# A two-layer LSTM scan with attention: the gates' biases written into PSUM by ScalarE instead of by nine bias matmuls a step

## The reference, cut to what matters

```
def _lstm_cell(x, h, c, Wi, Wh, bi, bh):
    g = x @ Wi.T + bi + h @ Wh.T + bh
    i, f, gg, o = jnp.split(g, 4, axis=-1)
    c2 = jax.nn.sigmoid(f) * c + jax.nn.sigmoid(i) * jnp.tanh(gg)
    h2 = jax.nn.sigmoid(o) * jnp.tanh(c2)
    return (h2, c2)
...
def step(carry, x_t):
    h0, c0, h1, c1, a = carry
    xin = jnp.concatenate([x_t, a], axis=-1)
    h0, c0 = _lstm_cell(xin, h0, c0, Wi0, Wh0, bi0, bh0)
    h1, c1 = _lstm_cell(h0, h1, c1, Wi1, Wh1, bi1, bh1)
    q = h1 @ Wq.T
    attn = jax.nn.softmax(jnp.einsum('bh,bsh->bs', q, context), axis=-1)
    mixed = jnp.einsum('bs,bsh->bh', attn, context)
    a2 = jnp.tanh(jnp.concatenate([mixed, h1], axis=-1) @ Wo.T + bo)
    return ((h0, c0, h1, c1, a2), a2)
```

## Time and profile before

| | |
|---|---|
| median of three runs | 8625.89 us |
| the profiled execution's own time | 8623.44 us |
| its span, first to last instruction | 8621.7 us |
| TensorE matmuls busy | 7757.2 us (90% of the span), 389701 instructions |
| VectorE busy | 4295.5 us (50%) |
| ScalarE busy | 2528.3 us (29%) |
| mean granted clock of TensorE | 0.969 |

### The profile page before, as it was taken

How to read it: one execution, slowest core, us unless ns; L and a number is a source line. 1 busy time by engine, 2 the same in 40 slices (tenths; PEclk the granted TensorE clock), 3 DMA queues, 4 the chain that set the end, 5 groups by cost and what they waited for, 6 DMA issues and landing times. The chain is left out here.

```text
span 8621.7 us, 829171 instructions
## 1 busy us (share of the span) xinstructions
PE 7757.2 (90%) x389701; PEld 6261.9 (73%) x389709; DVE 4295.5 (50%) x21178; ACT 2528.3 (29%) x12971; POOL 281.7 (3%) x295
## 2 busy tenths in 40 slices
PE   7999999999999999999999999999999999576677
PEld 5777777777777777777777777777777777353455
DVE  5444444444444444444444444444444444557712
ACT  2222222222222222222222222222222222223322
POOL 0000000000000000000000000000000000113411
PEclk8999999999999999999999999999999999798788
DMA  1000000000000000000000000000000000000233
GB/s 51 0 0 0 0 0 0 0 0 0 0 0 0 0 0 0 0 0 0 0 0 0 0 0 0 0 0 0 0 0 0 0 0 0 25 15 8 102 117 113
DMA packets 61677, 92.70 MB, mean 11 GB/s; under 512 B 13976, under 2 KB 50248, under 8 KB 60744
## 3 DMA queue, kind: packets, MB, share of 16 engines
q1 hardware_dynamic: 58568, 83.84, 2.9%
q0 software_dynamic: 3072, 8.39, 0.3%
HBM read 73.34 MB, written 18.87 MB: 11 GB/s over the span
## 5 line engine op out<-in xcount | busy, mean ns | idle before, releaser
L334 PE MATMUL scan_sums_ig<-rec_wh,scan_hT 128*8 128x64 f32 x65504 | 1291.2, 219 | 2.8 <-issue 2.8
L334 PEld LDWEIGHTS scan_sums_ig<-rec_wh,scan_hT 128*8 128x8 f32 x65504 | 1026.8, 90 | 3.2 <-issue 3.2
L456 DVE STREAM_TRANSPOSE scan_sums_f<-scan_sums_f 128x64 f32<-128x64 f32 x2048 | 543.3, 265 | 837.0 <-PE scan_sums_f L334 837.0
L405 ACT ACTIVATE scan_tanh_f<-scan_sums_f 128x8 f32<-128x8 f32 x2048 | 362.8, 177 | 1827.2 <-DVE scan_sums_f L456 1827.2
L334 PE MATMUL scan_sums_o<-rec_wh,scan_hT 128*4 128x64 f32 x32752 | 833.9, 219 | 3.0 <-issue 3.0
L334 PE MATMUL scan_sums_f<-rec_wh,scan_hT 128*4 128x64 f32 x32752 | 833.5, 219 | 0.0
L456 DVE STREAM_TRANSPOSE scan_sums_ig<-scan_sums_ig 128x64 f32<-128x64 f32 x2048 | 543.5, 265 | 372.2 <-PE scan_sums_ig L334 372.2
L334 PE MATMUL scan_sums_ig<-rec_wa,scan_aT 128*8 128x64 f32 x32768 | 646.7, 219 | 0.0
L334 PE MATMUL scan_sums_ig<-rec_wx,scan_xT 128*8 128x64 f32 x32768 | 645.8, 219 | 0.0
L334 PE MATMUL scan_sums_ig<-rec_wi,scan_hT 128*8 128x64 f32 x32768 | 645.0, 219 | 0.0
L419 ACT ACTIVATE scan_aT<-scan_a_sum 128x8 f32<-128x8 f32 x1024 | 181.5, 177 | 1510.6 <-DVE scan_a_sum L484 1510.6
(11 more groups left out here) (291 smaller groups left out, 14243.4 us busy)
## 6 DMA issues: line engine op xcount, KB each, us to landing
experts_bias<-in_b SPq DMA_DIRECT2D x40, 640.0 KB, 3.8
moe_w<-in_w SPq DMA_DIRECT2D x16, 1024.0 KB, 12.5
slots_x<-route_zero SPq DMA_DIRECT2D x40, 128.0 KB, 1.7
experts_x<-slots_x SPq DMA_DIRECT2D x40, 128.0 KB, 2.0
slots_y<-experts_y SPq DMA_DIRECT2D x40, 128.0 KB, 1.7
front_x<-in_x_steps SPq DMA_DIRECT2D x32, 128.0 KB, 2.0
w_xres<-in_x SPq DMA_DIRECT2D x4, 1024.0 KB, 9.8
out<-w_xres SPq DMA_DIRECT2D x8, 512.0 KB, 3.0
```

The lines of the kernel that those rows point to most:

```text
L334: last = nc.tensor.matmul(sums[layer][BANK[g]][32 * j:32 * j + ROWS[g], 0:64], state[:, k, FIRST[g]:FIRST[g] + ROWS[g]], weight[:, k, j, 6 ...
L405: nc.scalar.activation(tanh_f[l][:], gates_of[l][F][:, :, 0:B], ACT.Tanh).then_inc(f_tanh[l], 1)
L456: nc.vector.transpose(turned[l][g], sums[l][g][:, 0:64]).then_inc(gates_turned[l][g], 1)
```

## The change

The selection matrices, the bf16 parts and all nine seeds of a step are taken out. The three banks of a layer become one PSUM tensor, and ScalarE copies the layer's biases, laid out by the host in the shape of the sums (zero where no gate has a row), into the first 64 columns of all three banks with one instruction (`seed`). It does so right after its last tanh of the layer, once `hT` of that layer is there. TensorE waits for that copy (`seeded`) ahead of `wh1` and of `wh0`. Before the first step, six matmuls of zeros mark the banks as written, so that later products add onto ScalarE's data. The output's bias is added to `vp` once, in `prepare_scan` (the softmax's weights sum to one). With the seeds gone, `wx` of the input and cell gates also stands ahead of `vp`; only `wx` of the output gate is left behind it.

```diff
-                sp.wait_ge(rows_zeroed, 3)
-                for p in range(3):
-                    rows = slice(32 * p, 32 * p + 4)
-                    for l in range(2):
-                        gates = slice(BIAS_AT[l], BIAS_AT[l] + GATES)
-                        sp.dma_start(bias[0][rows, gates, :], ins[f"bi{l}"]).then_inc(bias_in, 16)
-                        sp.dma_start(bias[1][rows, gates, :], ins[f"bh{l}"]).then_inc(bias_in, 16)
-                    sp.dma_start(bias[0][rows, GATES, :], ins["bo"]).then_inc(bias_in, 16)
+                for l in range(2):
+                    for tile, name in ((bias[0], f"bi{l}"), (bias[1], f"bh{l}")):
+                        sp.dma_start(tile[:, l, :, :], ins[name]).then_inc(bias_in, 16)
+                sp.dma_start(bo[:], ins["bo"].partition_broadcast(P)).then_inc(bias_in, 16)
...
-                dve.wait_ge(bias_in, 16 * 15)
+                dve.wait_ge(bias_in, 16 * 5)
...
-                nc.vector.tensor_copy(w["bias_parts"][:], bias[0][:]).then_inc(parts, 1)
...
+                for at, gates in ((0, slice(0, 1)), (2, slice(3, 4))):
+                    nc.vector.tensor_scalar(w["bias"][:, :, at:at + 1, :], bias[0][:, :, gates, :], 0.5, None, ALU.mult).then_inc(scaled, 1)
+                nc.vector.scalar_tensor_tensor(w["bias"][:, :, 1, :], bias[0][:, :, 1, :], 0.5, bias[0][:, :, 2, :],
+                                               ALU.mult, ALU.add).then_inc(scaled, 1)
...
-                    nc.vector.tensor_copy(w["vp"][:, k, :, :].rearrange("p j u -> p (j u)"),
-                                          vp[k][:, 0:D]).then_inc(scaled, 1)
-                dve.wait_ge(scaled, 23)
+                    nc.vector.tensor_tensor(w["vp"][:, k, :, :].rearrange("p j u -> p (j u)"), vp[k][:, 0:D], bo[:],
+                                            ALU.add).then_inc(scaled, 1)
...
-        sums = [[m.psum(f"sums{l}_{g}") for g in ("f", "ig", "o")] for l in range(2)]
+        layer_sums = [m.psum(f"sums{l}", (P, 3, 512)) for l in range(2)]
+        sums = [[t[:, g, :] for g in range(3)] for t in layer_sums]
...
-                def seed_bias(bank, at, rows=w["sel"], start=True):
-
-                    nc.tensor.matmul(bank[:, 0:64], rows[:], bias_parts[:, 64 * at:64 * at + 64], start=start, stop=False,
-                                     skip_group_check=True)
-
-                def seed_gates(layer):
-                    at = BIAS_AT[layer]
-                    seed_bias(sums[layer][F], at + GATE_F)
-                    seed_bias(sums[layer][IG], at + GATE_I)
-                    seed_bias(sums[layer][O], at + GATE_O)
-                    seed_bias(sums[layer][IG], at + GATE_G, w["sel_high"], False)
...
+                    pe.wait_ge(seeded[1], n)
                     product(1, hT[1], w["wh1"])
                     pe.wait_ge(h_ready[0], n + 1)
                     product(1, hT[0], w["wi1"], done=gates_summed[1])
                     if not last:
-                        seed_gates(0)
+                        pe.wait_ge(seeded[0], n + 1)
                         product(0, hT[0], w["wh0"], (GATE_F, GATE_I, GATE_G))
                     pe.wait_ge(h_ready[1], n + 1)
                     head_product(scores, state_of(hT[1]), w["kp"], True, True).then_inc(scores_done, 1)
-                    seed_bias(a_sum, GATES)
-                    head_product(a_sum, state_of(hT[1]), w["woh"], False, False)
+                    head_product(a_sum, state_of(hT[1]), w["woh"], True, False)
                     if not last:
                         product(0, hT[0], w["wh0"], (GATE_O,))
-                        seed_gates(1)
                         pe.wait_ge(x_ready, n + 1)
-                        product(0, xT[(s + 1) % 2], w["wx"], (GATE_F,))
+                        product(0, xT[(s + 1) % 2], w["wx"], (GATE_F, GATE_I, GATE_G))
                     pe.wait_ge(probs_ready, n)
                     head_product(a_sum, pT[:], w["vp"], False, True).then_inc(a_summed, 1)
                     if not last:
-                        product(0, xT[(s + 1) % 2], w["wx"], (GATE_I, GATE_G, GATE_O))
+                        product(0, xT[(s + 1) % 2], w["wx"], (GATE_O,))
                 pe.wait_ge(zeroed, 1)
-                seed_gates(0)
-                seed_gates(1)
+                for l in range(2):
+                    for bank in sums[l]:
+                        last = nc.tensor.matmul(bank[:, 0:64], w["ident"][:], zeros[:], start=True, stop=True, skip_group_check=True)
+                    last.then_inc(opened, 1)
+                pe.wait_ge(seeded[0], 1)
                 pe.wait_ge(x_ready, 1)
                 product(0, xT[0], w["wx"])
                 with pe.Fori(0, T // U - 1) as i:
...
+                def seed(l, n):
+
+                    act.wait_ge(h_ready[l], n)
+                    nc.scalar.activation(layer_sums[l][:, :, 0:64], w["bias"][:, l, :, :], ACT.Copy).then_inc(seeded[l], 1)
...
                         nc.scalar.activation(tanh_c[l], c_of[l], ACT.Tanh).then_inc(h_factors[l], 1)
+                        seed(l, n + 1)
...
-                act.wait_ge(zeroed, 1)
+                act.wait_ge(opened, 2)
+                for l in range(2):
+                    seed(l, 1)
...
+    def bias_rows(bias):
+
+        rows = np.zeros((4, 32, GATES, 64), bias.dtype)
+        for g, first in enumerate((0, 0, B, 0)):
+            rows[:, first:first + B, g, :] = gate_blocks(bias)[g][:, None, :]
+        return rows.reshape(P, GATES, 64)
```

More of the change, by code:

```diff
@@ L120, in prepare_scan @@
         ctx_split = m.sbuf("ctx_split", [P, KC, 2, P])
[L122 to L125, removed]
+        bias = [m.sbuf(f"bias{i}", [P, 2, GATES, 64]) for i in range(2)]
+        bo = m.sbuf("bo", [P, D])
         kp = [m.psum(f"kp{k}") for k in range(2)]
         vp = [m.psum(f"vp{k}") for k in range(2)]
-        zeroed, ident_done, rows_zeroed = m.sem("zeroed"), m.sem("ident_done"), m.sem("rows_zeroed")
+        zeroed, ident_done = m.sem("zeroed"), m.sem("ident_done")
         fold_in, scan_in, bias_in = m.sem("fold_in"), m.sem("scan_in"), m.sem("bias_in")
-        folded, scaled, parts = m.sem("folded"), m.sem("scaled"), m.sem("parts")
+        folded, scaled = m.sem("folded"), m.sem("scaled")
         with nc.Block() as block:
@@ L159, in _ @@
                                             channel_multiplier=1).then_inc(zeroed, 1)
[L161 to L164, removed]
                 pool.wait_ge(zeroed, 6)
@@ L312, in scan @@
         xT = [m.sbuf(f"xT{i}", [P, 2, 3 * B]) for i in range(2)]
+        zeros = m.sbuf("zeros", [P, 64])
         state_of = lambda tile: tile[:, :, B:2 * B]
@@ L323, in scan @@
                                "inv_done", "a_turned", "a_kept", "zeroed"))
+        opened = m.sem("opened")
+        seeded = [m.sem(f"seeded{l}") for l in range(2)]
         with nc.Block() as block:
@@ L326, in _ @@
             def _(pe):
-                bias_parts = w["bias_parts"][:].rearrange("p g u -> p (g u)")
                 def product(layer, state, weight, gates=(GATE_F, GATE_I, GATE_G, GATE_O), done=None):
@@ L446, in _ @@
                     nc.vector.memset(tile[:], 0.0)
+                nc.vector.memset(zeros[:], 0.0)
                 nc.vector.memset(scores[:, 0:S], 0.0)
@@ L1531, in build @@
                         r[name] = m.sbuf(name, [P, 2, 4, 64])
-                    r["bias_parts"] = m.sbuf("bias_parts", [P, BIASES, 64], BF16)
-                    r["sel"] = m.sbuf("sel", [P, P], BF16)
-                    r["sel_high"] = m.sbuf("sel_high", [P, P], BF16)
+                    r["bias"] = m.sbuf("bias", [P, 2, 3, 64])
                     r["off_rows"] = m.sbuf("off_rows", [P, 1])
@@ L1609, in lay_out @@
         "woh": wo[:, D:].reshape(4, 64, 4, 2, 32).transpose(2, 4, 3, 0, 1).reshape(P, 2, 4, 64),
-        "bo": a["L0_xattn_bo"].reshape(4, 64),
+        "bo": a["L0_xattn_bo"],
         "w_in": chunked(a["L0_ffn_W_in"].T),
@@ L1624, in lay_out @@
     for name in ("bi0", "bh0", "bi1", "bh1"):
-        out[name] = bias_blocks(a[f"L0_xattn_{name}"])
+        out[name] = bias_rows(a[f"L0_xattn_{name}"])
     return {k: np.ascontiguousarray(v) for k, v in out.items()}
```

8 lines of the change are left out of this document (1 added, 7 removed).

## The result

The changed kernel took 8551.06 us (median of four runs, 8549.21 to 8551.91) against 8628.57 us (8621.46 to 8632.06): a ratio of 0.991, with a 95% interval of 0.9895 to 0.9926. 8545 was forecast.

A forecast was written before the change was run, and what follows sets the result against it. The recurrence was taken to bound the kernel, not TensorE. From the profiled 8623.4 us, 77 for covered branches and 3 for preparation and start gave 8543, stated as 8545 us; own range 8532 to 8560, 8-in-10 range 8528 to 8608.

The forecast's parts named there:

- What bounds the kernel: Scan: the recurrence's chain sets a step's length, not TensorE; removing the seeds by itself puts 0 on the path.
- The branch: TensorE's loop end: uncovered branch makes aT wait, 0.151 us each; moving wx ahead of vp covers it fully.
- The size: Scan: 511 branches at 0.151 us each, 77 us saved; 55 us by the skill's 108 ns.
- ScalarE's copies: Scan, after each layer's last tanh: about 0.35 us each, covered, cost 0 unless a copy took over 0.72 us.
- Preparation and start: Ahead of the first step: -3 us together, bounds -5 to 0, with zero matmuls and two copies adding some 1 us.
- VectorE's part: Preparation: VectorE's work on the biases shrinks to 1.5 us for all, 4 us less.
- The room ahead of `vp`: TensorE between kp and vp: with two more wx gates, loads end by 4006.43 against vp at 4006.87, covered by 0.4 us.
- VectorE's branch: VectorE's loop end behind a_hist: taken as covered; if late by up to 0.15 us, it eats up to the whole gain.
- Their writes: Rival, chance 0.04: ScalarE's writes hold TensorE during copies; whole-copy holds add 717 us, about 9260; 0.037 us each undoes the gain.
- The clock: Rival, chance 0.04: TensorE busy falls to 83%, clock drops; a lower-level step costs about 1.5 us more, all 10,100 us.

The follow-up runs named there:

- one-gate kernel: Kernel before, all nine seeds kept, only wx of the input gate moved from behind vp to ahead of it: 8557.06 us, ratio 0.9923.
- old order: Changed kernel (seeds gone, ScalarE's copies in), but wx of the input and cell gates behind vp as before: 8616.96 us, ratio 0.9989.
- bf16 kernel: Changed kernel with the six opening matmuls of zeros in bf16 in place of f32: 8547.32 us, ratio 0.9905.
- two gates early: Kernel before, all nine seeds kept, wx of forget, input and cell gates ahead of vp, output gate behind: 8671.16 us, ratio 1.0053.

## Why the prediction was right, step by step

**What bounds the kernel** was right: the recurrence and not TensorE, shown by the one-gate kernel, whose seeds all stayed, and by the old order, which had none and gained 3 us of 7322 in the scan.

**The branch** was right in mechanism. Its excess is gone; uncovered the branch is 0.23 us, at the low end of the 0.23 to 0.28 that I had read. The Trainium skill's 108 ns for a compare-and-branch ("Advanced Engine Details and Errata", Control Flow Timing) is for that instruction alone; here it comes with a register instruction, and the measurement decides.

**The size:** 77 us were forecast for the scan, 64.9 came. The excess went whole, but it was smaller than I took it: the 0.151 us came from ten steps of each kind, and over the scan it is 0.140, so 72 us and not 77. The other 6 us are that a step became 7.086 us where one inside the body was 7.080. It isn't from ScalarE's copies (7.084 with twice as many, and 7.081 inside the body of the old order, which has them too), nor from work behind `vp` (7.081 and 7.085 with none). The kernel of before with VectorE's loop of four has 7.086 inside its body as well, and the one with one gate early 7.076. What sets these 10 ns between kernels stays open.

**Preparation and start:** the term was -3 us, and +0.4 came up to the first tanh. VectorE's part is as costed:

```profile
22.11 0.69 DVE L168 TENSOR_TENSOR prep_bias<-prep_bias 128x512 f32<-128x512 f32 x1 [22.11 <-DMA prep_bo<-in_bo]
22.83 0.36 DVE L171 TENSOR_SCALAR rec_bias<-prep_bias 128x128 f32<-128x128 f32 x2
...
23.32 0.69 DVE L99 TENSOR_SCALAR rec_wx<-rec_wx 128x1024 f32<-128x1024 f32 x1
```

The scaling of the weights starts at 23.32 in place of 27.96 us, 4.6 us earlier. TensorE's first matmul of the scan starts only 2.9 us earlier, 78.11 against 81.00; the other 1.7 us are lost in `turn_inputs`, and why is open. (That matmul starts anywhere from 77.0 to 78.5 us in the five kernels with the f32 opening, so part of this may be chance.) The start of the scan in the kernel before:

```profile
81.00 0.10 PEld L350 LDWEIGHTS scan_sums_f<-rec_bias_parts,rec_sel 128*128 128x128 bf16 x1 [3.57 <-DVE scan_pT L452]
...
81.54 0.32 PEld L334 LDWEIGHTS scan_sums_f<-rec_wx,scan_xT 128*4 128x4 f32 x16
```

From there to `wx` it was 0.5 us, and it is 3.7 now: the zero matmuls take 2.8 us at a granted clock of 0.50, ScalarE's two copies follow and only then `wx`. So the opening costs 3.2 us more and not the 1 that I gave. This is the term that was mis-sized, and the bf16 kernel takes 2.3 us of it back.

**Behind the scan** 7.1 us were gained that no step of the prediction names. The kernels without seeds take 1199.4 to 1204.6 us there and those with them 1207.8 to 1212.5, but for the one with TensorE's loop of four, which keeps its seeds and takes 1204.6. The cause is open.

The errors cancel in part: +12, +3 and -7 us around the sum of 8543, which gives 8551. That the forecast came within 6 us is some luck, since the 7 us belong to no step of it.

**The room ahead of `vp`** (ending 0.4 us early) was right, 4005.84 + 0.72 = 4006.56 against 4007.03. **VectorE's branch** lay under its wait, as taken. **ScalarE's copies** cost nothing, as predicted: inside the body a step is 7.081 us with them (old order) and 7.080 without. Their writes don't hold TensorE: `wi1`'s 64 loads take 0.89 us beside a copy, as `wa`'s do with none. **The clock** stayed at 1.00 with TensorE busy 5.87 of 7.09 us, 83% as forecast. What the Trainium skill tells of micro-idling between groups ("TensorE: Matmul & The Clock Gate", A second HAM failure mode: psum-queue depth-cycling) didn't happen at gaps of 0.16 to 0.39 us between its matmuls, four in a step.

## What to carry to other kernels

Count the waits, not only their sum: an engine that waits for its input in every second step and not in the others has something at its loop's end that nothing hides. Put the branch where the engine waits anyway, behind as little work as the links ahead of it allow; here a single gate's product, moved, does it. And work taken off an engine that the recurrence waits past gives nothing but room: ask what that room makes possible, and test the move without the removal.

## What the chip showed that I had not expected

A loop body of two steps on TensorE ran 511 times without fetching an instruction; one of four fetched 213 KB in every iteration and the kernel went from 8626 to 13237 us. The Trainium skill, "Advanced Engine Details and Errata", ISA Cache, gives TensorE 128 KB, and an estimate from the measured 213 KB for four steps gives a body of two some 106 KB. The traces agree with the page on both sides.

A bf16 seed over the whole array, 0.20 us by its row, costs more than that between `kp` and `woh`, whose matmuls load 4 columns each. From `kp`'s first load to `woh`'s it is 0.48 us with the seed between (two gates early) and 0.17 us without (after): 0.31 us for one.
